# Three of a chunk's four projections in one step, two of them in banks of the scores; token products one step sooner

## The reference

```
Q, K = x Wq', x Wk'   (16 heads of 64)      V = x Wv'   (16 heads of 16)
dl = x Wdl' (12 levels a head)   g = -exp(A_log) * softplus(x Wdt' + dt_bias)
Lam = softplus(Lp * dl)          cg = cumsum(g over tokens)
W[t,s] = (Q_t . K_s / 8) * exp(cg_t - cg_s) * Lam[t, level(t xor s)]   for s <= t, else 0
o = layernorm(W V Wout' + x) * ln_g + ln_b ;  x1 = layernorm(x + o)
two gated steps with c (sigmoid, sigmoid, tanh; wf wi wc uf ui uc), h = tanh(x1 wo' + c uo' + bo)
out = layernorm(x1 + h)
```

## Time and profile before

| | us |
|---|---|
| median of 3 runs | 700.78 (699.0 to 701.05) |
| the profiled execution, its own time | 703.26 |
| its span in the profile | 701.5 |
| TensorE busy | 670.3 (96%) |
| VectorE, GpSimd, ScalarE busy | 475.2, 355.5, 339.6 |

### The profile page before, as it was taken

The page is one execution under the profiler, slowest core; times in us unless marked ns, Lnnn a source line. Parts: engine busy times, 40 slices in busy tenths (PEclk is TensorE's granted clock), DMA queues, the critical chain, the costliest instruction groups (busy, mean ns, idle before and its releaser), DMA issues.

```text
span 701.5 us, 22072 instructions
## 1 busy us (share of the span) xinstructions
PE 670.3 (96%) x9172; PEld 603.3 (86%) x9172; DVE 475.2 (68%) x1067; ACT 339.6 (48%) x759; POOL 355.5 (51%) x476
## 2 busy tenths in 40 slices
PE   5889999999999999999999999999997999999994
PEld 3779999998999999899999999999986788888894
DVE  2843768688776968675877769686877445454546
ACT  4545455544444453555444444545443434555555
POOL 1652755645564646466565636565464224344434
PEclk9989999999999999999999999999999899999997
DMA  8020312203050402112150503121222000000002
GB/s 296 26 57 18 80 40 58 68 31 96 3 95 7 92 21 78 35 33 64 35 95 3 95 9 90 35 63 49 35 66 93 1 1 0 31 32 31 30 31 91
DMA packets 53588, 37.09 MB, mean 53 GB/s; under 512 B 5360, under 2 KB 52080, under 8 KB 53488
## 3 DMA queue, kind: packets, MB, share of 16 engines
q1 hardware_dynamic: 53488, 35.67, 20.2%
HBM read 30.41 MB, written 5.24 MB: 51 GB/s over the span
## 4 chain that ended last, share of the span: by engine, by line
PE 88%; DVE 3%; DMA 2%; POOL 2%; ACT 2%; SPq 1%; issue 1%; DVEq 0%; ACTq 0%
PE bank L378 64%; PE bank L381 6%; PE bank L467 5%; PE bank L400 5%; PE bank L432 4%; PE bank L496 4%; SPq L325 1%; DMA xt<-in_wffn 1%; DMA bv<-in_bcv 1%; DVE t L966 1%; ACT t L735 1%; POOL wL L1333 1%; POOL t L1333 0%; DVE ng L963 0%; DVE t L963 0%
## 5 line engine op out<-in xcount | busy, mean ns | idle before, releaser
L378 PE MATMUL bank<-xH,wH 128*128 128x256 f32 x480 | 148.3, 309 | 2.4 <-ACT KT L735 1.1
L378 PE MATMUL bank<-xL,wH 128*128 128x256 f32 x480 | 136.1, 284 | 0.0
L378 PE MATMUL bank<-xH,wL 128*128 128x256 f32 x480 | 135.5, 282 | 0.0
L735 ACT ACTIVATE QT<-bank 128x512 f32<-128x512 f32 x64 | 38.2, 597 | 144.1 <-PE bank L378 144.1
L963 DVE TENSOR_TENSOR W<-bank,E 128x512 f32<-128x512 f32 x128 | 82.2, 684 | 35.6 <-PE bank L378 35.6
L378 PEld LDWEIGHTS bank<-xH,wH 128*128 128x128 f32 x480 | 91.4, 190 | 10.2 <-issue 9.0
L378 PEld LDWEIGHTS bank<-xL,wH 128*128 128x128 f32 x480 | 91.7, 191 | 0.4
L378 PEld LDWEIGHTS bank<-xH,wL 128*128 128x128 f32 x480 | 91.7, 191 | 0.0
L735 ACT ACTIVATE E<-bank 128x512 f32<-128x512 f32 x128 | 66.1, 603 | 17.4 <-PE bank L400 17.4
L378 PE MATMUL bank<-QT,KT 64*128 64x128 f32 x1024 | 65.9, 279 | 0.6 <-ACT E L735 0.6
L735 ACT ACTIVATE KT<-bank 128x512 f32<-128x512 f32 x64 | 38.0, 594 | 54.1 <-PE bank L378 54.0
(11 more groups left out here) (149 smaller groups left out, 1660.5 us busy)
## 6 DMA issues: line engine op xcount, KB each, us to landing
cB<-scr SPq DMA_DIRECT2D x240, 64.0 KB, 3.0
xt<-in_xT SPq DMA_DIRECT2D x16, 256.0 KB, 3.7
xs<-in_x SPq DMA_DIRECT2D x16, 256.0 KB, 4.1
out<-xs SPq DMA_DIRECT2D x16, 256.0 KB, 2.1
xt<-in_wffn SPq DMA_DIRECT2D x8, 256.0 KB, 3.2
QT<-in_wqk SPq DMA_DIRECT2D x4, 256.0 KB, 5.8
KT<-in_wqk SPq DMA_DIRECT2D x4, 256.0 KB, 6.9
scr<-cT SPq DMA_DIRECT2D x16, 64.0 KB, 1.9
```

Source lines behind the costliest of these rows:

```text
L378: return e.matmul(o, a, b, start=start, stop=stop)
L735: return e.activation(o, i, f, **kw)
```

## The change

Of a pair's eight projections, P(0) now stands at the end of step 0, P(1) to P(3) together at the end of step 2, P(4) at the end of step 4 and P(5) to P(7) together at the end of step 6; steps 1, 3, 5 and 7 have none. Counted from the chunk they run beside, a pair's first projection is one step later than before. Of each three the first is in bank 0, the second and third are in banks 1 and 2, which are the first two of the scores' banks; they wait for the first half of the chunk's weights (`d_w`), and `exponents` waits in turn for their drain (`a_qk`). The token products (j = 0, 1) move from step 5 to step 4, ahead of the scores; softplus and the other jobs stay in their steps. `turn_coefs` moves from step 5 to step 6 (a new job number 6), behind the projections, and with it the copy on ScalarE, `load_coefs` on SyncE and the order of jobs in `MISC`. `STEPS` begins one step sooner, for the tokens of pair 1.

```diff
--- before.py
+++ after.py
@@ -39,14 +39,14 @@
 
 
 
-STEPS = range(-3, NG + 13)
+STEPS = range(-4, NG + 13)
 FIRST_FFN = NG - 1
 
 
 def token_jobs(s):
 
     out = []
-    for d, j in ((12, 7), (0, 0), (0, 1), (1, 2), (3, 8), (5, 3), (7, 4), (8, 5)):
+    for d, j in ((12, 7), (1, 2), (3, 8), (5, 3), (7, 4), (8, 5), (9, 6), (-1, 0), (-1, 1)):
         n = s + 11 - d
         if n % 8 == 0 and (0 if j == 7 else 1) <= n // 8 < NSG:
             out.append((n // 8, j))
@@ -54,8 +54,13 @@
 
 
 def project_jobs(s):
-    sg, j = (s + 9) // 8, (s + 9) % 8
-    return [(sg, j)] if 1 <= sg < NSG else []
+
+    sg, n = (s + 8) // 8, (s + 8) % 8
+    return [(sg, j) for j in {0: [0], 2: [1, 2, 3], 4: [4], 6: [5, 6, 7]}.get(n, [])] if 1 <= sg < NSG else []
+
+
+
+PROJECT = [0, 0, 1, 2, 0, 0, 1, 2]
 
 
 def chunk_at(s, d):
@@ -81,7 +86,7 @@
     for sg, j in token_jobs(s):
         if j == 3:
             out += [("cgt", sg, 0)]
-        if j == 5:
+        if j == 6:
             out += [("cft", sg, 0)]
     for sg, j in token_jobs(s):
         if j == 0:
@@ -90,8 +95,8 @@
 
 
 MISC = {}
-for _s in range(-4, NG):
-    for _job in misc_jobs(_s) if _s > -4 else [("tok", 0, 0), ("tok", 0, 1), ("cgt", 0, 0), ("cft", 0, 0)]:
+for _s in range(-5, NG):
+    for _job in misc_jobs(_s) if _s > -5 else [("tok", 0, 0), ("tok", 0, 1), ("cgt", 0, 0), ("cft", 0, 0)]:
         MISC[_job] = (len(MISC) % 2, len(MISC) // 2)
 
 INTER = {ci: n for n, ci in enumerate([c for c in range(NC) if c % CB])}
@@ -394,6 +399,8 @@
                 e.wait_ge(g_at, ci + 1)
                 if ci:
                     e.wait_ge(d_w, 4 * ci)
+
+                e.wait_ge(a_qk, min(4 * ci + 8, 8 * NSG))
                 for j in range(4):
                     for q in range(4):
                         r = slice(32 * q, 32 * q + 32)
@@ -560,7 +567,7 @@
                     y.then_inc(p_tok, 1)
 
             def project(sg, j):
-                b, Q, q = sg % 2, banks[0], j % 2 == 0
+                b, Q, q = sg % 2, banks[PROJECT[j]], j % 2 == 0
                 m0 = j if q else 8 + j - 1
                 e.wait_ge(g_xl, sg)
                 if sg == 1:
@@ -569,7 +576,13 @@
                         e.wait_ge(d_wl, 3 + 2 * (j % 2))
                     else:
                         e.wait_ge(g_wl, 2 + 2 * (j % 2))
-                e.wait_ge(a_qk, 8 * sg + j)
+                if PROJECT[j]:
+
+                    e.wait_ge(d_w, 8 * (sg - 1) + j // 4 * 4 + 2)
+                elif j:
+                    e.wait_ge(a_qk, 8 * sg + {1: 1, 4: 2, 5: 5}[j])
+                else:
+                    e.wait_ge(a_qk, 8 * sg - 2 if sg > 1 else 8)
                 for i in range(2):
                     c = slice(128 * (m0 + i), 128 * (m0 + i) + 128)
                     for k in range(2):
@@ -748,7 +761,7 @@
                     act(wH[:, k, c], w0[k][:, c], ACT.Copy).then_inc(a_wh, 1)
 
             def project(sg, j):
-                n = 5 * (j % 2) if sg == 0 else 0
+                n = 5 * (j % 2) if sg == 0 else PROJECT[j]
                 b, q = sg % 2, j % 2 == 0
                 m0 = j if q else 8 + j - 1
                 src = banks[n][:, :].rearrange("p (m t) -> p m t", m=2)
```

## The result

The changed kernel takes 718.25 us in the median of 4 runs (717.78 to 719.42) against 700.1 of before: ratio 1.0253, 95% interval 1.0229 to 1.0277, 2.5% slower. The profiled execution has a span of 717.6 us (own time 719.42) against 701.5, so 16.1 us are to be explained where I had forecast 4.4 (the medians lie 18.2 apart, as the profiled execution of before was one of its longer ones).

What follows compares the result with a forecast made beforehand. TensorE's own queue was taken to bound the kernel, busy 99.70 of 100 us. Terms -4.8 + 4.7 + 0.8 + 1.1 + 2.6 = +4.4 us gave a median of 705.2 us, range 698.0 to 710.0.

Steps and rivals of the forecast that it cites:

- the chain that I named for decays: Even chunks: decays wait for VectorE's product, which waits for cB, late behind the turn; 0.5 us in twelve chunks, +4.7 net.
- the end: SyncE's queue: last coefficients' trip 2.6 us later, FFN weight loads behind it, so last scores later: +2.6, bounds +1.5 and +5.
- chunk 29: Four projections where it had three, less the idle time ahead of exponents(30): +1.1 us.
- the start: One projection more at half clock between decays(1) and exponents(1): +0.8 us, bounds -0.7 and +2.6.
- Joints: TensorE's switches between products: grouping saves 0.11 us a chunk; an odd chunk saves 0.38 in all, thirteen give -4.8.
- With one level stall 0.5 to 0.6, with two 0.3 to 0.4: Ahead of decays in even chunks, by late cB; taken as 0.5 us (bounds 0 and 0.9) for twelve chunks.
- 8.6 for the way from cT to cB: From cT's end: 1.97 trip to memory, seven issues of 0.52, 3.0 to land; cB there at E + 8.25.
- What feeds an even chunk shifts with the tokens and with the chunk's end alike, so I take VectorE as late there as before: VectorE in even chunks, after tokens move a step sooner: yt done by E + 6.9, ahead of out_proj at E + 7.1.
- decays find their bank free: Rival: in even chunks VectorE ends its first product by E + 8.1, no stall at decays; 699.2 us, chance 0.22.
- The group does not run together: Rival: exponents' drain or a weights' bank stalls TensorE 0.2 us in each of 28 chunks; 710.8 us, chance 0.08.

Runs made afterwards that it cites:

- the turn and normalise moved: The changed kernel with the turn ahead of the three projections of step 6 and normalise ahead of the tokens, decays where the change has them: 696.39 us.
- all three moves: The changed kernel with the turn ahead of the projections, decays behind the projections of step 2 and normalise ahead of the tokens: 696.13 us.
- decays behind: The changed kernel with decays behind the three projections of step 2 instead of ahead of them, on TensorE alone: 708.53 us.
- normalise ahead: The changed kernel in which VectorE issues normalise ahead of token jobs 0 and 1 of the same step, not behind them: 720.1 us.
- the turn alone: The kernel before with only the turn of the coefficients, its copy and load_coefs one step later, behind step 6's one projection: 703.59 us.
- the extra operation: The kernel before with one more GpSimd addition in each chunk, behind its work for the levels, into a tile that nobody reads: 709.88 us.
- the tokens sooner alone: The kernel before with only the token products one step sooner, in step 4 ahead of the scores: 706.58 us.

## Why the prediction was wrong

The sign was right and the chain that I named for decays is there; the size was short by 11.7 us of span, and 718.25 lies outside the range of 698.0 to 710.0. Two terms failed in the steady chunks, the stall ahead of decays in its size and VectorE's place in even chunks outright. By parts, measured less forecast: even chunks +9.5, odd chunks +2.7, the end +2.7, chunk 29 -0.1, the start -3.0. That the start came out lower hides part of the miss, and I can't claim it.

- **Joints, right.** Odd chunks without a new wait gained 0.31 to 0.36 us against 0.37 (the items add up to 0.38), even ones without any wait 0.19 (14.58 before, 14.39 with the turn and normalise moved) against 0.11; one price of 0.2 for every switch had given 0.2. State is followed by exponents after 1.04 (416.14 to 417.18 in the run with turn and normalise moved), so that joint costs no more than state to P, where I took 0.06 more; tokens to scores take 0.3 where I took 0.21. The group runs without gaps, as I said, and with all three moves the odd chunks do gain 4.4 us against my 4.8.
- **"With one level stall 0.5 to 0.6, with two 0.3 to 0.4", mis-sized.** The eight chunks lost 1.06 each where the sum had 0.39: 5.4 us more. Decays waited 0.48 to 1.50 us in them, 1.01 in the mean. The failed number is 8.6 for the way from cT to cB, which was 9.26 in the mean, so that cB landed 8.8 behind exponents and not 8.25, which is about what the stall grew by. For the kernel before 8.6 was nearly right (8.69 in the mean, 9.28 at most), though by the page's median of 3.0 to land where the last of eight counts; only its slowest trip comes up to the 9.26. Why the trips are longer stays open: the means of the thirteen runs lie between 8.69 and 9.50, that of before is the lowest of all, and no run takes this apart. With two levels it is less in three of four chunks, as I had it (6, 10 and 22 lost 0.52 to 0.90, those with one level 0.94 to 1.35), but chunk 26, whose trip took 9.83, lost 1.56.
- **"What feeds an even chunk shifts with the tokens and with the chunk's end alike, so I take VectorE as late there as before", wrong.** This is the step that failed outright: 3.9 us beyond the forecast in five even chunks (5.4 lost, 1.6 forecast), and the gain of 0.37 in each of five odd ones and 0.5 in chunk 15, 6.2 us together. I had named normalise as what stands behind the tokens and costed it by TensorE's need alone. What hangs on it is GpSimd, which waits for oo, and whose work then falls on VectorE's additions and makes them 1.41 us longer in chunk 23. VectorE began the first S<-S of chunk 24 at E + 0.84 in place of E + 0.14, and the keys waited 0.75. The prediction reads no row of GpSimd.
- **The end, mis-sized:** 5.3 us for 2.6, just past the upper bound of 5. The trip was issued at 528.03, 0.27 ahead of exponents(30), as forecast. Then VectorE waited 3.1 us for cB, state 1.53 for VectorE's product, exponents(31) 3.55 (3.80 before) and the last scores 2.00 for ScalarE's E (0.60 before). From exponents(30) to its first wait in the gated steps TensorE stands for 8.0 us in place of 5.1. The remaining 2.3 us fall where the clock is lower: over the 40 us from 540 it was granted 0.79, over those from 528 before 0.87, both 2 us ahead of exponents(31). The late turn brings this loss: from exponents(30) on the four runs in which the turn stands behind the projections of step 6 (after, decays behind, normalise ahead, the turn alone) take 188.6 to 189.9 us, the nine others 183.2 to 186.8. The last scores do wait for a weight, as forecast, since ScalarE makes E right behind it:

```profile
548.31 0.63 ACT L748 ACTIVATE wH<-xt 128x512 fp32r<-128x512 f32 x1 [4.25 <-DMA xt<-in_wffn]
```

- **The start, wrong sign:** -2.2 for +0.8. TensorE idled 5.75 us ahead of decays as forecast (some 6), and yet the low clock ended sooner: the longer idle time did not prolong it, as I had taken it to. Granted clock, 40 to 50 and 50 to 60 us, of after:

```profile
40.00:50.00 10.00, 4.88 (x25) 4.88 (x26) 7.43 (x12) 0.89 (x2) 4.75 (x5) 0.66 0.01 2
50.00:60.00 10.00, 10.00 (x148) 9.28 (x148) 2.79 (x5) 6.88 (x20) 2.39 (x5) 1.00 0.01 2
```

  In the kernel before the two stretches have a granted clock of 0.78 and 0.71.
- Of the rivals, "decays find their bank free" is what the turn ahead of the projections brings about. "The group does not run together" had nothing behind it but the 0.8 us ahead of exponents(16), where I had 0.6.

## What to carry to other kernels

When a block that stands between a producer and the next user of its bank is moved away, list every instruction that then comes to stand there: decays, the turn and the tokens each waited for the product behind inter, and each needed another cover or another place. Follow a moved step through every queue down to the engine that has most idle time, because what it does later may fall on another engine's operations without any semaphore showing it. And give a chain with a trip through memory a range from many trips, not one number: here single trips lay 1.4 us apart in one kernel, and the mean moved by 0.6 from the kernel before to the one after. Put its head (here the turn) in front of whatever can wait.

## What the runs showed of the hardware

- A VectorE addition with both inputs in SBUF stood until GpSimd's running operation was over, and ended 0.28 us later: 0.42 became 0.86, 1.39 (after) and 1.17 (the extra operation). No wait row shows it, only the longer duration. Two S<-S of 0.35 each took 2.29 us in the midst of GpSimd's softplus in after, ending 0.21 us behind one of its operations each. In these chunks operations that read a PSUM bank kept their durations (zt out of the bank 1.02 for two beside GpSimd's).
- The low clock at the start doesn't go by the idle time in front of it alone. Decays(1) came after 3.05 us of idle time in the kernel before, and exponents(2) 26.3 us later (45.59 to 71.88); with the tokens sooner alone after 3.06 us, and exponents(2) 23.2 us later (43.99 to 67.19); in the kernel after behind 5.75 us, and 24.6 us later (45.12 to 69.67). What sets how long the low clock lasts stays open, and with it my term for the start. Some microseconds of the times of the single parts come from there, so I read them by their chunks.
- The granted clock can fall behind idle times of very different lengths. The extra operation delays xL at the start, TensorE stands 2.44 us at 34.04 where it stood 1.00 at 31.05 before, and the granted clock falls a first time there, ahead of the drop that the kernel before and after have; with normalise ahead of the tokens it fell behind 1.45 and 2.21 us, and not behind 2.07. Stretches of the run with the extra operation:

```profile
30.00:40.00 10.00, 7.56 (x41) 6.39 (x43) 5.85 (x7) 2.58 (x8) 5.88 (x7) 0.83 0.29 82
50.00:60.00 10.00, 8.77 (x68) 8.12 (x68) 7.28 (x15) 2.15 (x4) 2.22 (x2) 0.58 0.01 2
```

  In the kernel before they have 1.00 and 0.71. Of the 5.5 us by which exponents(2) come later, 3.0 are there by 34.04, ahead of the first drop; 1.5 come between it and decays(1), and 1.0 behind.
